# A four-layer model in one launch on one core: the delta rule's order, the stages around it, and an attention over heads as one pipeline of token tiles

## The reference

```python
h = rmsnorm(x, norm_in_w)
h = silu(causal_conv4(h) + conv_b)            # per channel
q, k, v = h @ q_w, h @ k_w, h @ v_w           # 16 heads of 64, q and k of unit length
alpha, beta = sigmoid(h @ alpha_w + alpha_b), sigmoid(h @ beta_w + beta_b)
def step(s, inp):                             # one token
    qt, kt, vt, at, bt = inp
    s = s * at[..., None]
    u = einsum('bhd,bhdv->bhv', kt, s)
    s = s + bt[..., None, None] * (kt[..., None] * (vt - u)[..., None, :])
    return s, einsum('bhdv,bhd->bhv', s, qt)
y = rmsnorm(outs) * head_norm_w
gate = sigmoid(silu(x @ u1_w + u1_b) @ u2_w + u2_b)
y = x + y @ out_w * gate
y = y + silu(rmsnorm(y) @ ff_w1) * (rmsnorm(y) @ ff_w3) @ ff_w2
```

```python
q = rope((x @ Wq + bq).reshape(B, T, 16, 8)); k, v = split((x @ Wdown + bdown) @ Wup + bup)
scores = q . rope(k) * 8 ** -0.5              # for each token a 16x16 matrix over h, g
out = softmax(scores over g) @ v              # (16, 8) for each token
y = out @ Wout + bout
```

## Time and profile before

| | |
|---|---|
| median of 3 runs | 6820.89 us (6817.22 to 6825.5) |
| the profiled execution | 6872.23 us; its span 6870.4 us, mean granted clock 0.869 |
| busy in the span: TensorE, VectorE, GpSimd, ScalarE | 78%, 50%, 37%, 34% |
| delta input | 1859.0 to 2041.8 us: 182.8 us |
| delta rule | 2041.9 to 4759.9 us: 2718 us |
| delta output | 4763.8 to 5040.4 us: 276.6 us |
| last attention | 5780.5 to 6328.4 us: 547.9 us |
| all other stages (three attention layers' parts and four feed-forward layers) | not touched by the change |

### The profile page before, as it was taken

The page is one execution under the profiler, slowest core; times in us unless marked ns, Lnnn a source line. Parts: engine busy times, 40 slices in busy tenths (PEclk is TensorE's granted clock), DMA queues, the critical chain, the costliest instruction groups (busy, mean ns, idle before and its releaser), DMA issues.

```text
span 6870.4 us, 180526 instructions
## 1 busy us (share of the span) xinstructions
PE 5324.7 (78%) x70660; PEld 3956.2 (58%) x70660; DVE 3447.2 (50%) x9349; ACT 2368.9 (34%) x4122; POOL 2561.7 (37%) x2842
## 2 busy tenths in 40 slices
PE   4568758888719999999999999997579996111998
PEld 3434435555417877787777787786246664101676
DVE  4531357777634444444444444444445555676433
ACT  3432236666523333333333333333223332000333
POOL 2210014444315555555555556554100002675000
PEclk8789879999859899999999999998789998555999
DMA  0000000000000000000000000000010000000000
GB/s 17 0 17 0 2 37 1 0 0 0 0 6 12 11 11 11 11 11 11 11 11 12 11 10 11 11 13 11 0 37 0 0 0 3 0 0 25 0 0 12
DMA packets 29512, 57.41 MB, mean 8 GB/s; under 512 B 7312, under 2 KB 14240, under 8 KB 28704
## 3 DMA queue, kind: packets, MB, share of 16 engines
q1 hardware_dynamic: 28960, 48.86, 2.2%
HBM read 46.75 MB, written 2.10 MB: 7 GB/s over the span
## 4 chain that ended last, share of the span: by engine, by line
PE 52%; DVE 9%; POOL 3%; another core or an unknown queue 3%; issue 2%; ACT 1%; DVEq 0%; POOLq 0%; ACTq 0%
PE psum L617 7%; PE psum L607 7%; PE psum L2055 5%; PE psum L2026 5%; PE psum L2069 3%; PE psum L600 3%; PE psum L2167 2%; PE psum L2151 2%; PE psum L2161 2%; DVE e_sq L2470 2%; PE psum L2043 1%; POOL a_pv L1480 1%; PE psum L2202 1%; PE psum L2182 1%
## 5 line engine op out<-in xcount | busy, mean ns | idle before, releaser
L617 PEld LDWEIGHTS psum<-m_wd,m_h 128*128 128x128 f32 x6144 | 812.8, 194 | 485.3 <-issue 484.1
L617 PE MATMUL psum<-m_wd,m_h 128*128 128x128 f32 x6144 | 825.5, 278 | 91.2 <-remote 64.4
L1914 POOL TENSOR_TENSOR e_kd<-e_kd,e_tail 128x512 f32<-128x512 f32 x325 | 369.5, 1137 | 694.1 <-PE psum L2026 680.8
L607 PE MATMUL psum<-xT,m_wa 128*128 (+1 forms) x1032 | 552.7, 618 | 8.5 <-remote 8.5
L607 PE MATMUL psum<-xT,m_wb 128*128 (+1 forms) x1032 | 540.4, 606 | 0.0
L784 DVE SCALAR_TENSOR_TENSOR m_acc<-psum,m_combine,m_acc 128x128 f32<-128x128 f32 x1440 | 403.4, 342 | 223.3 <-PE psum L617 209.5
L544 POOL TENSOR_TENSOR m_h<-m_td,m_tb 128x512 f32<-128x512 f32 x258 | 328.5, 1273 | 487.1 <-DVE m_tb L812 487.1
L2055 PEld LDWEIGHTS psum<-e_T,e_N 64*64 64x64 f32 x10400 | 336.0, 137 | 217.6 <-issue 216.6
L2026 PE MATMUL psum<-e_kd,e_k 64*64 64x64 f32 x10400 | 375.7, 223 | 49.4 <-DVE e_AT L2418 49.3
L2055 PE MATMUL psum<-e_T,e_N 64*64 64x32 f32 x10400 | 371.9, 222 | 43.6 <-remote 43.6
L2026 PEld LDWEIGHTS psum<-e_kd,e_k 64*64 64x64 f32 x10400 | 343.5, 138 | 57.8 <-issue 56.4
(11 more groups left out here) (412 smaller groups left out, 11727.5 us busy)
## 6 DMA issues: line engine op xcount, KB each, us to landing
e_w<-in_e_w SPq DMA_DIRECT2D x66, 321.0 KB, 2.8
m_wa<-in_m_wa SPq DMA_DIRECT2D x12, 512.0 KB, 7.2
m_wd<-in_m_wd SPq DMA_DIRECT2D x12, 512.0 KB, 8.7
m_wb<-in_m_wb SPq DMA_DIRECT2D x8, 512.0 KB, 9.0
f_h<-in_f_h SPq DMA_DIRECT2D x2, 1024.0 KB
out<-x SPq DMA_DIRECT2D x1, 2048.0 KB, 8.7
f_w<-in_f_w SPq DMA_DIRECT2D x3, 256.0 KB
g_w<-in_g_w SPq DMA_DIRECT2D x3, 256.0 KB
```

What stands on the lines that cost most here:

```text
L607: pe.matmul(c.ps[i][:], w[q][:, j, :], xb, start=True, stop=True).then_inc(a_ready[i], 1)
L617: r = pe.matmul(c.ps[4 + e % 2][:, t * P:(t + 1) * P], h[:, u % DEPTH, t * P:(t + 1) * P], wd[u // UQ][:, u % UQ, :], start=(m == 0 and t ...
L1914: return g.tensor_tensor(both_odd(dst[:], m), both_odd(src[:], m), gate.unsqueeze(1).broadcast_to((P, 2, nb, m)), ALU.mult)
```

## The change

Four functions change; the diff's core is shown per function.

**Delta rule.** `z_step(l)` and `scaled_gram(l + 1)` become one function, called five times; with l = 5 it takes in `cross_gram`. Per chunk it issues z of head 0, z of head 1, gram of head 0, gram of head 1. Z of head h is now written to the other half of the partitions, and read back by ScalarE for head 0 and VectorE for head 1:

```diff
-    UNROLL = 5
+    UNROLL = 13
+            def z_and_gram(l):
+                ... (waits: n_ready, t_ready, lv_ready, gr_free)
+                for u in range(NC):
+                    for h in range(2):
+                        r = pe.matmul(c.psum[half(1 - h), Z_, u * HC:(u + 1) * HC], N[half(h), l - 1, chunk(u)],
+                                      even(T[half(h), chunk(u)], 1 << l), start=True, stop=True)
+                        if u + 1 == NC:
+                            r.then_inc(z_ps[h], 1)
+                    if l + 1 < LEVELS:
+                        r = gram_chunk(l + 1, k, kd, u)
+                    elif u % 2:
+                        r = cross_block(u // 2)
+                r.then_inc(gr_ps, 1)
             def z_copy():      # ScalarE
-                a.activation(flat(Z), c.ps[Z_][:, 0:NC * HC], ACT.Copy).then_inc(z_ready, 1)
+                a.activation(flat(Z[half(0)]), c.psum[half(1), Z_, 0:NC * HC], ACT.Copy).then_inc(z_ready[0], 1)
+            def z_copy():      # VectorE
+                v.tensor_copy(flat(Z[half(1)]), c.psum[half(0), Z_, 0:NC * HC]).then_inc(z_ready[1], 1)
```

```diff
+            for b in range(B):                     # VectorE
+                if b + 1 < B: third(b + 1)         # second norm's application
+                if b + 2 < B: first(b + 2)         # statistics of x
+                conv(b)
+                if b + 2 < B: second(b + 2)        # first norm's application, second's statistics
+                if b >= 1: betas(b - 1)
```

**Delta output.** Straight code in two phases. First, for all 8 batches: norm, transposes, u1, silu, u2, sum. Then one sigmoid over 128x4096 elements. Then the gating on GpSimd (product and sum, formerly VectorE's) and the feed-forward part:

```diff
+            turn_sums(0); up(0); turn_sums(1)      # TensorE; up: eight matmuls of 512 columns
+            for b in range(B):
+                if b + 1 < B: up(b + 1)
+                if b + 2 < B: turn_sums(b + 2)
+                down(b)                            # 16 matmuls with w2
```

**Last attention.** Straight code over N = 32 tiles. GpSimd forms three of four q-k products and two of four p-v products of a tile, VectorE the others. The sums are matmuls with the identity; the value sums have the product as weights, so that the result comes out transposed, and the transposes of `o` go:

```diff
+            def score_sums(n):     # TensorE
+                for d in range(HD):
+                    r = pe.matmul(c.ps[4 + n % 2 * 3][:, 0:H * H], c.ident[:], prod[:, n % 2, :, d],
+                                  start=(d == 0), stop=(d == HD - 1))
+            def value_sums(n):
+                for g in range(H):
+                    r = pe.matmul(c.ps[5][:, t * P:(t + 1) * P], pv[:, n % 2, g, :, :].rearrange("p h d -> p (h d)"),
+                                  c.ident[:], start=(g == 0), stop=(g == H - 1))
+            for n in range(N + 1):                 # TensorE
+                if n + 1 < N: score_sums(n + 1)
+                if n: value_sums(n - 1)
+                ... (project and expand of batch b + 1 at n % 4 == 0, output(b - 1) at 1, turn_input(b + 2) at 3)
+            for n in range(N):                     # VectorE
+                normalise(n); values(n)            # sum, reciprocal and product of the softmax; two of four p-v products
+                if n + 2 < N: scores(n + 2)        # one of four q-k products
+                if n + 1 < N: centre(n + 1)        # maximum and subtraction, out of PSUM
+                ... (finish(b - 2) at n % 4 == 0, rotate(b + 1) and result(b - 1) at 1, input_stats(b + 2) at 2)
+            for n in range(N + 1):                 # ScalarE
+                ... (copy_sums(b - 1) and copy_latent(b + 1) at n % 4 == 0)
+                if n + 1 < N: exps(n + 1)
+                ... (input_norm(b + 2), copy_input(b + 2) and result_norm(b - 1) at 3)
```

More of the change, by code:

```diff
@@ L1433, in stage_attn3 @@
[L1433 to L1443, removed]
@@ L1764, in _ @@
+            conv_in(0)
+            for b in range(B):
+                if b + 1 < B:
+                    conv_in(b + 1)
+                silu(b)
+            a.wait_ge(b_ready, 1)
+            a.sem_clear(b_ready)
+            a.activation(c.beta[:], bt[:].rearrange("p (t h) a -> p a t h", h=2), ACT.Sigmoid)
         @block.vector
@@ new lines, in betas @@
+            def betas(b):
+                i = b % 2
+                v.wait_ge(b_ps[i], 1)
+                v.sem_clear(b_ps[i])
+                r = v.tensor_tensor(bt[:, b * NC:(b + 1) * NC, :], c.ps[6 + i][:, 0:NC * NPAIR].rearrange("p (u a) -> p u a", u=NC),
+                                    bb[:].unsqueeze(1).broadcast_to((P, NC, NPAIR)), ALU.add)
+                r.then_inc(b_read[i], 1)
+                return r
+            first(0)
+            second(0)
+            third(0)
+            first(1)
@@ L1795, in stage_delta_in @@
+            second(1)
+            for b in range(B):
+                if b + 1 < B:
+                    third(b + 1)
+                if b + 2 < B:
+                    first(b + 2)
+                conv(b)
+                if b + 2 < B:
+                    second(b + 2)
+                if b >= 1:
+                    betas(b - 1)
+            betas(B - 1)
+            v.drain().then_inc(b_ready, 1)
     st.ctx.close()
@@ new lines, in _ @@
+            turn_input(0)
+            for b in range(B):
+                if b + 1 < B:
+                    turn_input(b + 1)
+                gate_up(b)
+                if b:
+                    gate_down(b - 1)
+            gate_down(B - 1)
+            pe.sem_clear(y_ready)
+            for i in range(2):
+                pe.wait_ge(x_read[i], 1)
+                pe.sem_clear(x_read[i])
+                pe.wait_ge(g2_read[i], 1)
+                pe.sem_clear(g2_read[i])
+            turn_sums(0)
@@ L2644, in _ @@
+            up(0)
+            turn_sums(1)
+            for b in range(B):
+                if b + 1 < B:
+                    up(b + 1)
+                if b + 2 < B:
+                    turn_sums(b + 2)
+                down(b)
             for i in range(2):
@@ L2675, in _ @@
+            copy_sums(0)
+            for b in range(B):
+                silus(b)
+                if b + 1 < B:
+                    copy_sums(b + 1)
         @block.vector
@@ new lines, in _ @@
+            gate_sum(B - 2)
+            gate_sum(B - 1)
+            sums_stats(0)
+            sums_norm(0)
+            sums_stats(1)
+            hidden(0)
+            sums_norm(1)
+            sums_stats(2)
+            for b in range(B):
+                if b + 1 < B:
+                    hidden(b + 1)
+                if b + 2 < B:
+                    sums_norm(b + 2)
+                if b:
+                    finish(b - 1)
+                result(b)
+                if b + 3 < B:
+                    sums_stats(b + 3)
```

969 lines of the change are left out of this document (555 added, 414 removed).

## The result

The changed kernel takes 6466.96 us (median of 4 runs, 6448.49 to 6483.2) against 6823.19 us before (4 runs, 6817.22 to 6829.8): a ratio of 0.9477, 95% interval 0.9448 to 0.9505. Forecast were 6243 us, range 6125 to 6440. The direction is right and the time lies 27 us above the range. The profiled run has a span of 6481.4 us, 389 less than before; forecast were 582 less. So a third of the forecast gain is missing in the profiled execution.

What follows compares the result with a forecast made beforehand. TensorE bounds the delta rule; waits between engines bound the other three stages. Delta rule -251, delta input -88, delta output -85, attention -158 sum to -582: 6872 to 6290, less 0.75% gives 6243 us, range 6125 to 6440.

Steps and rivals of the forecast that it cites:

- Score sums: Last attention: a record of 256 columns read with a 32-byte step takes TensorE 0.22 us, 3.5 us a tile.
- the strided read costs double: Rival, last attention: TensorE takes 12.6 us a tile instead of 9.1, 60 to 85 us more, 6315 us; 15%.
- TensorE stays at the lower clock: Rival, last attention: 17 us of TensorE a tile, stage 585 us, 6436 us in all; 6%.
- Two waits: Delta output, wide part: TensorE waits 1.9 us for the norm and 1.2 for VectorE's sums, within 14.8 a batch.
- Delta rule, the merge: Z and gram calls in merged groups of 0.95 us; five merges save 4.7 us a step.
- No overlap of four: Rival, delta rule: merged Z and gram as slow as in two groups, 305 us more, 6546 us; 12%.
- A start floor: Rival, delta rule: a minimum time between matmul starts adds 211 us, 6452 us; 4%.
- Slower than before: Rival, delta rule: calls changing quadrant wait for each other's end, 7.4 us a merged group, 8330 us; 4%.
- Delta rule, the waits: TensorE's waits in a full-clock step rise from 2.75 to 4.4 us, at places listed along the new order.
- Unrolling: Delta rule, 5 to 13 steps a round: 12 loop ends become 4 at 7 us each, -56 us.
- the likeliest case: Whole kernel: the main forecast of 6243 us, with 6150 to 6340 as its own range; 50%.
- waits as before and the attention at 340: The case "Better than I say", delta rule and last attention: 6120 us; 9%.

Runs made afterwards that it cites:

- e1: The changed kernel with score-sum matmuls reading 256 neighbouring elements instead of every eighth, so summing other elements, for timing only: 6374.5 us.
- e6: The changed kernel with two delta output orders altered: GpSimd's gated sum ahead of its root, VectorE's gate sum one batch later: 6400.7 us.
- e4: The changed kernel with Z and gram calls as two loops, first Z, then gram, instead of alternating: 6718.9 us.
- e5: The changed kernel with Z of each head written to its own partition half again, calls still alternating with the gram: 6836.8 us.
- e8: The changed kernel with diagonal() back between cross_z() and cross_t() in the delta rule: 6462.2 us.
- e9: The changed kernel with UNROLL = 5 in the delta rule, so 12 loop ends instead of 4: 6530.3 us.
- e13: The changed kernel with z_and_gram(1) moved between solve(0) and state_and_output(0) in the delta rule: 6630.2 us.

## Why the prediction was wrong, by its own steps

**Score sums.** "Ends: 0.22 a record as for packed columns, 0.45, ... I take the first, being the same instruction otherwise." It was the other end, 0.46, and the rival "the strided read costs double" (15%) is what happened: it gave 60 to 85 us more, e1 shows 92. This is the step that I should have taken otherwise, as no row of such a read spoke for the lower end.
The Trainium skill's lines of 16 bytes ("SBUF — State Buffer", in the part on Door 1) pointed to the upper end, as the prediction itself says.
With a packed read the stage takes 359 us from first to last instruction, some 366 as the 458 is counted, against my 390. So the rest of this sum was too large by 24 us, and it hid that much of the miss. Its terms were on the careful side, though one was set low by a slip: five waits of half a GpSimd instruction (1.28 to 1.50 us) are 3.2 to 3.8 us, not 2.7. The rival that TensorE stays at the lower clock falls, its granted clock is 0.95 here.

**Delta output.** "Two waits" a batch was the failing count, 14.8 us. I added up each engine's work and the waits that follow a product, and did not walk the order once round all engines. The 4.15 us wait for GpSimd's gating behind its own root, and TensorE's lower clock that follows, are the third term; the gate part's 5.2 us a batch "at the lower clock" took TensorE for the bound where the loop of 8.4 us was. e6 brings back 66 us, nearly all that was missing. There is a slip as well: 188 against 277 is 89 less, and the sum has 85.

**Delta rule, the merge.** Right: four run together, through the four quadrants (e4, e5). Sized at 4.7, it brought 4.3. "No overlap of four", "A start floor" and "Slower than before" fall: 64 records start in 0.99 us, 15 ns apart.

**Delta rule, the waits.** The places were right: cross_t, state_and_output(0), from_state, t_step(1), groups 3 and 4 all stop. Their idle time is 3.66 us, less than my 4.4. What failed is that the new order was priced by the idle time alone; 1.20 us a clean step lie in the records before the stops and in the other groups. The merge's 0.4 comes on top, and 0.7 less of idle time goes off: 0.8 us over 35.1, 52 us. Of the waits that I listed one costs nothing, the 0.75 of cross_t, since GpSimd's scaling bounds the way from gram 0 to gram 1 (e8). The other 23 us of 75 are steps behind a loop end, which with five steps a round average 42.4 us before and 42.5 in e9: the new order brought them nothing, and I had counted all 65 alike.

**Unrolling.** -56 forecast, -57 between e9 and the changed kernel in the steps' sum, -63 in the time. The loop end was priced rightly. **Delta input.** -88 forecast, -92.

**The step from the profile to the median.** The profiled execution was forecast at 6290 us and took 6483.2: 193 of the 224 us. The other 31 lie in the last step, "the median of the runs shown, 6820.9, is 0.75% under the profiled one". That held for one execution before the change. The changed kernel's median is 0.25% under its profiled run, 16 us where I had taken off 47. With 0.75% the time would have been 6435, just inside the range.

**The range.** Three misses of 66 to 69 us went one way. I had given them single rivals and a range of the likeliest case, as if only one could come true: the strided read alone (6315) and the out-of-range 6467 are 152 us apart, and that is the other two and the step to the median. At the other end "waits as before and the attention at 340" is 107 + 50 us less, 6087 and not 6120; nothing hung on it.

## What to carry to other kernels

Lay data out for the engine that reads it as a matmul's operand: steps of 16 and 32 bytes doubled TensorE's time, while the strided write that avoids it cost GpSimd nothing and VectorE 0.3 us a product, 4 us in the stage against 92. When a pipeline is reordered over several engines, walk its order once round, from an engine back to itself, and take the longest such loop; the sum of one engine's work is only a lower bound. Before a stop is filled, ask what bounds the stretch around it: e8 filled one that cost nothing, and e13 uncovered a wait of 2.19 us to fill one of 0.56. By the traces' starts a stop of a busy TensorE takes up to 0.2 us beside its idle time, which no run has tested. Where TensorE is short of work the lower clock behind a wait can cost about as much as the wait (5.51 us of idle time in the delta output, then three pairs of matmuls at 1.9 to 2.1 us instead of 1.0).

## What the hardware showed that was not expected

- Float32 matmul reads with steps of 4, 8, 16 and 32 bytes: 216, 227, 453 and 460 ns for a record of 256 columns at full clock. At the lower clock the first two take 427, and the other two what they take at full clock, so there TensorE's clock does not set the pace.
- Two pairs of 64x64 matmuls in all four quadrants: 64 records in 0.99 us; in two quadrants 1.91 us for the same 64.
- A write of 128x512 elements with a step of 1 KB: no cost on GpSimd (1477 against 1481 ns), 1.02 instead of 0.68 us on VectorE (shortest of 32).
- TensorE at the lower clock from the delta rule's first gram 0 to its last matmul: 375 us before, 314 after, 454 in e4 and 584 in e5. Why e5 has most stays open.
